# Own slots for ScalarE's reads, value heads stored by group, keys loaded in parts: a two-stage attention block

## What is computed

```python
x = x + _L0_conv_ref(_gn(x), L0_conv_qkv_w, L0_conv_rpb, L0_conv_proj_w, L0_conv_proj_b)
t = _to_tokens(x)
t = t + _L1_attn_ref(_ln_t(t), L1_attn_Wq, L1_attn_bq, L1_attn_Wk, L1_attn_bk, L1_attn_Wv, L1_attn_bv, L1_attn_Wo, L1_attn_bo)
t = t + _L1_ffn_ref(_ln_t(t), L1_ffn_qidx, L1_ffn_scales, L1_ffn_W)
x = _from_tokens(t, x)
```

```python
scores = jnp.einsum("bhqd,bhkd->bhqk", q, k) * scale
weights = jax.nn.softmax(scores, axis=-1)
attn = jnp.einsum("bhqk,bhkd->bhqd", weights, v)
```

## Time and profile before

| | us |
|---|---|
| timed runs, median of 3 | 9913.16 |
| timed runs, lowest and highest | 9905.24, 9916.07 |
| the profiled execution | 9896.01 |
| its span, first to last instruction | 9894.2 |
| front of image 0, alone | 0 to about 486 |
| images 0 to 7 start at | 607, 1774, 2975, 4189, 5390, 6596, 7804, 9012 |

### The profile page before, as it was taken

One profiled execution on the slowest core, in us unless ns is written; L12 is line 12 of the kernel. 1 busy time (PEld: TensorE's weight loads), 2 busy tenths in 40 slices (PEclk: granted clock), 3 DMA queues, 4 the chain that ended last, 5 costly groups with the idle time before them and its releaser, 6 DMA issues.

```text
span 9894.2 us, 433953 instructions
## 1 busy us (share of the span) xinstructions
PE 8886.0 (90%) x173506; PEld 4454.4 (45%) x173506; DVE 7894.2 (80%) x14135; ACT 6501.4 (66%) x13345; POOL 1827.8 (18%) x1913
## 2 busy tenths in 40 slices
PE   4679999999999999999999999999999999999998
PEld 3434444444444444444444444444444444444553
DVE  4478888888887888788888888878888788888996
ACT  1236666666676666666667666666666666667777
POOL 4402221022211222012220122201222022220000
PEclk8779999999999999999999999999999999999999
DMA  3331112211122111221113111121111311112000
GB/s 58 61 53 27 33 35 40 46 31 33 32 38 48 33 31 32 47 39 32 32 35 56 25 33 33 35 53 32 31 31 34 58 29 31 34 29 45 8 10 8
DMA packets 499353, 354.25 MB, mean 36 GB/s; under 512 B 105820, under 2 KB 489036, under 8 KB 495308
## 3 DMA queue, kind: packets, MB, share of 16 engines
q1 hardware_dynamic: 497356, 325.95, 18.4%
HBM read 233.15 MB, written 78.05 MB: 31 GB/s over the span
## 4 chain that ended last, share of the span: by engine, by line
PE 78%; issue 10%; DVE 6%; ACT 3%; SPq 2%; POOL 1%; DVEq 0%; DMA 0%; ACTq 0%; POOLq 0%
PE PS L943 21%; PE PS L1020 19%; PE PS L1005 19%; PE PS L773 6%; PE PS L815 6%; PE PS L824 4%; DVE block_max L1448 3%; PE PS L834 2%; ACT PB L1221 1%; SPq L564 1%; DVE PVM L1333 1%; ACT tail L1141 1%; PE PS L797 0%; POOL SC L682 0%; DVE SUMS L1323 0%
## 5 line engine op out<-in xcount | busy, mean ns | idle before, releaser
L1221 ACT ACTIVATE PB<-PS 128x448 f32<-128x448 f32 (+1 forms) x11200 | 5471.3, 544 | 2532.6 <-PE PS L1005 2508.3
L1448 DVE TENSOR_REDUCE block_max<-PS 128x1 f32<-128x448 f32 x10878 | 6146.8, 616 | 926.9 <-PE PS L943 861.2
L943 PE MATMUL PS<-KP,QP 96*32 96x448 bf16 x43904 | 4199.0, 360 | 238.5 <-issue 106.1
L1005 PE MATMUL PS<-QP,KP 99*32 99x448 bf16 x43904 | 4216.5, 356 | 92.9 <-issue 49.6
L1020 PE MATMUL PS<-PB,VA 128*32 128x448 f32 x22400 | 2698.1, 545 | 34.6 <-issue 32.8
L943 PEld LDWEIGHTS PS<-KP,QP 96*32 96x32 bf16 x43904 | 1291.4, 96 | 1979.6 <-DVE block_max L1448 837.2
L1005 PEld LDWEIGHTS PS<-QP,KP 99*32 99x32 bf16 x43904 | 1309.2, 97 | 1311.4 <-issue 572.0
L1020 PEld LDWEIGHTS PS<-PB,VA 128*32 128x32 f32 x22400 | 736.6, 111 | 399.4 <-issue 63.9
L682 POOL TENSOR_TENSOR SC<-SC,NM 128x1120 f32<-128x1120 f32 x224 | 461.9, 2062 | 2034.7 <-DVE NM L1319 2034.7
L687 POOL TENSOR_TENSOR SC<-SC,SUMS 128x1120 f32<-128x1120 f32 x224 | 462.0, 2062 | 1990.2 <-DVE SUMS L1328 1990.2
L815 PE MATMUL PS<-Kn,QB 32*32 32x80 f32 x25088 | 622.9, 237 | 204.7 <-issue 76.8
(11 more groups left out here) (99 smaller groups left out, 3801.0 us busy)
## 6 DMA issues: line engine op xcount, KB each, us to landing
VP<-vT_padded SPq DMA_DIRECT2D x1792, 70.0 KB
KP<-k_dram SPq DMA_DIRECT2D x96, 392.0 KB, 13.6
QP<-q_dram SPq DMA_DIRECT2D x672, 56.0 KB, 2.1
k_dram<-k_parts SPq DMA_DIRECT2D x56, 336.0 KB, 4.8
q_dram<-q_parts SPq DMA_DIRECT2D x56, 336.0 KB, 3.1
VA<-v_dram SPq DMA_DIRECT2D x16, 816.0 KB, 22.7
vT_padded<-VTs SPq DMA_DIRECT2D x112, 112.0 KB
out_y<-X SPq DMA_DIRECT2D x56, 224.0 KB, 2.0
```

The costliest lines, as they stand in the source:

```text
L943: ins = mm(PS[at:at + QT, bank, 0:BLK], QP[0:ROWS, Q_SLOTS[k % AUNITS], t:t + QT], KP[0:ROWS, g, t // BLK, j * BLK:(j + 1) * BLK], start=T ...
L1005: ins = mm(PS[k0:k0 + 32, bank, 0:BLK], KP[0:ROWSM, k // NBLK, h, c * P + k0:c * P + k0 + 32], QP[0:ROWSM, Q_SLOTS[k], h * BLK:(h + 1) * B ...
L1221: S.activation(exp_buffer(k, c)[0:n, h, :], PS[0:n, at % ST_BANKS, 0:BLK], ACT.Exp, scale=float(ADIM) ** -0.5).then_inc(exp_done, 1)
L1448: V.tensor_reduce(block_max[:, q, j:j + 1], PS[:, bank, 0:BLK], AX.X, ALU.max).then_inc(max_read, 1)
```

## The change

Four edits, most of them in the Plan and in SP's program:

1. negate_max moves from slot (t + 22, 0) to (t + 21, 1) and invert from (t + 2, 0) to (t + 1, 1): the slots in which PE runs turn_max and spread.
2. The DRAM copy of the value heads gets the group as its outermost dimension. store_v2 writes each group by itself (4 DMAs instead of 2 per block; a partition's run in DRAM is 3 x 68 columns, in SBUF it is three pieces of 68). load_v reads one run of 24 x 68 columns (6528 bytes) per partition, instead of 24 pieces of 272 bytes.
3. The keys of group 0 of a new image are loaded in 7 parts (load_k0), one per block of 448 tokens, each of 6 DMAs of 64 rows of 896 bytes; a part stands at least 4 slots behind the key product of its block and at slot 179 + 5 j or later, and waits for the landing of store_k(j).
4. The keys of group 1 are loaded in 6 parts (load_k1), one per stacked part, at slots 4, 14, 24, 34, 44 and 54 instead of all at 2.

```diff
@@ class Plan
-                    self.fix(t + MAX_CHUNKS + 1, 0, "negate_max", k + 1)
+                    self.fix(t + MAX_CHUNKS, 1, "negate_max", k + 1)
...
-                self.fix(2, 0, "load_k", 1)
+                for n in range(len(K_PARTS)):
+                    self.fix(4 + 10 * n, 1, "load_k1", n)
                 self.fix(2, 0, "load_v", 1)
...
             self.fix(t + 1, 1, "spread", k)
-            self.fix(t + 2, 0, "invert", k)
+            self.fix(t + 1, 1, "invert", k)
...
             self.fix(t + 3, 0, "store_k", j)
+            self.fix(max(t + 4, NBLK * CHUNKS + 4 + 5 * j), 1, "load_k0", j)
...
-        self.fix(t + 4, 1, "load_k", 0)
-        self.fix(t + 4, 1, "load_v", 0)
+        self.fix(t + 5, 1, "load_v", 0)
@@ SP
-    v_dram = nc.dram_tensor("v_dram", (images, P, CHUNKS, GROUPS, VCOLS), F32, kind="Internal").ap()
+    v_dram = nc.dram_tensor("v_dram", (images, GROUPS, P, CHUNKS, VCOLS), F32, kind="Internal").ap()
...
                 def store_v2(j):
...
-                    sp.dma_start(dst[:, c + whole[0]:c + whole[1], :],
-                                 VS[:, whole[0]:whole[1], :, :].rearrange("p c h e -> p c (h e)")).then_inc(v_out, 16)
...
+                    for g in range(GROUPS):
+                        dst = image_of(v_dram, b, ahead)[:, g, :, :, :].rearrange("b p c e -> (b p) c e")
+                        heads = slice(g * GH, (g + 1) * GH)
+                        sp.dma_start(dst[:, c + whole[0]:c + whole[1], :],
+                                     VS[:, whole[0]:whole[1], heads, :].rearrange("p c h e -> p c (h e)")
+                                     ).then_inc(v_out, 16)
...
-                def load_k(g):
-                    of_image = ahead if g == 0 else 0
-                    wait(sp, k_out, of(b, of_image, 16 * NBLK, 16 * NBLK))
+                def load_k0(j):
+                    arrived(k_out, of(b, ahead, 16 * NBLK, 16 * (j + 1)))
                     if ahead == 1:
-                        wait(sp, st_ready, of(b, 0, AUNITS * GH * CHUNKS, (1 - g) * NBLK * GH * CHUNKS))
+                        arrived(st_ready, of(b, 0, AUNITS * GH * CHUNKS, NBLK * GH * CHUNKS))
                     for n, m in enumerate(K_PARTS):
-                        src = image_of(k_dram, b, of_image)[:, m, g * GH * ADIM:(g + 1) * GH * ADIM, :] \
+                        src = image_of(k_dram, b, ahead)[:, m, 0:GH * ADIM, j * BLK:(j + 1) * BLK] \
                             .rearrange("b (h e) t -> e (b h) t", e=ADIM)
-                        sp.dma_start(KP[n * ADIM:(n + 1) * ADIM, g, :, :], src).then_inc(keys_in[g], 16)
+                        sp.dma_start(KP[n * ADIM:(n + 1) * ADIM, 0, :, j * BLK:(j + 1) * BLK], src).then_inc(keys_in[0], 16)
+
+                def load_k1(n):
+                    arrived(k_out, of(b, 0, 16 * NBLK, 16 * NBLK))
...
+                    sp.dma_start(KP[n * ADIM:(n + 1) * ADIM, 1, :, :], src).then_inc(keys_in[1], 16)
...
                 def load_v(g):
...
-                    sp.dma_start(dst[:, 0:CHUNKS - 1, :], src[:, 0:CHUNKS - 1, g, :]).then_inc(heads_in[g], 16)
...
+                    cut = (CHUNKS - 1) * VCOLS
+                    sp.dma_start(VA[:, g, 0:cut], src[:, 0:cut]).then_inc(heads_in[g], 16)
```

More of the change, by code:

```diff
@@ L348, in wait @@
                 eng.wait_ge(s, value)
-            if eng is nc.sync and not isinstance(value, int):
-                apart(eng)
         def apart(eng):
@@ L450, in _, with arrived @@
         def _(sp):
+            def arrived(s, value):
+                wait(sp, s, value)
+                if not isinstance(value, int):
+                    apart(sp)
             def load(dst, src):
@@ L511, in store_v1 @@
                     if j == 0:
-                        wait(sp, pv_in, of(b, ahead, STRIPS, 0))
-                    wait(sp, vT_out, of(b, ahead, 32 * NBLK, 32 * j))
-                    wait(sp, v1_read, of(b, ahead, NBLK, j + 1))
+                        arrived(pv_in, of(b, ahead, STRIPS, 0))
+                    arrived(vT_out, of(b, ahead, 32 * NBLK, 32 * j))
+                    arrived(v1_read, of(b, ahead, NBLK, j + 1))
                     for r in range(2):
@@ L521, in load_windows @@
                     row = window_row(s)
-                    wait(sp, vT_out, of(b, ahead, 32 * NBLK, 32 * ((row + WI - 1) // BLOCK_ROWS + 1)))
-                    wait(sp, pv_in, of(b, ahead, STRIPS, s))
+                    arrived(vT_out, of(b, ahead, 32 * NBLK, 32 * ((row + WI - 1) // BLOCK_ROWS + 1)))
+                    arrived(pv_in, of(b, ahead, STRIPS, s))
                     for ky in range(WI):
@@ L535, in store_v2 @@
                 def store_v2(j):
-                    wait(sp, v2_read, of(b, ahead, NBLK, j + 1))
+                    arrived(v2_read, of(b, ahead, NBLK, j + 1))
                     c = 7 * j // 2
@@ L539, in store_v2 @@
                     rows = slice(0, P // 2) if j % 2 == 0 else slice(P // 2, P)
-                    dst = image_of(v_dram, b, ahead).rearrange("b p c g e -> (b p) c (g e)")
-                    sp.dma_start(dst[:, c + whole[0]:c + whole[1], :],
-                                 VS[:, whole[0]:whole[1], :, :].rearrange("p c h e -> p c (h e)")).then_inc(v_out, 16)
-                    sp.dma_start(dst[rows, c + half:c + half + 1, :],
-                                 VS[rows, half:half + 1, :, :].rearrange("p c h e -> p c (h e)")).then_inc(v_out, 16)
@@ L546, in load_k @@
-                def load_k(g):
-                    of_image = ahead if g == 0 else 0
-                    wait(sp, k_out, of(b, of_image, 16 * NBLK, 16 * NBLK))
+                    for g in range(GROUPS):
[4 more added lines that the diff above has]
+                                     ).then_inc(v_out, 16)
+                        sp.dma_start(dst[rows, c + half:c + half + 1, :],
+                                     VS[rows, half:half + 1, heads, :].rearrange("p c h e -> p c (h e)")
+                                     ).then_inc(v_out, 16)
@@ L594, in store_out @@
                 def store_out(i):
-                    wait(sp, ffn_out, of(b, third(i), NBLK, i + 1))
+                    arrived(ffn_out, of(b, third(i), NBLK, i + 1))
                     dst = image_of(yv, b, third(i)).rearrange("b c t -> (b c) t")
@@ L609, in do @@
                         store_v2(i)
-                    elif task == "load_k":
-                        load_k(i)
+                    elif task == "load_k0":
+                        load_k0(i)
+                    elif task == "load_k1":
+                        load_k1(i)
                     elif task == "load_v":
@@ L631, in _ @@
                         do(task, i)
-            do("load_k", 1)
+            for n in range(len(K_PARTS)):
+                do("load_k1", n)
             do("load_v", 1)
@@ L1361, in v2 @@
                     dve.wait_ge(v2_in, of(b, ahead, NBLK, j + 1))
-                    wait(dve, v_out, of(b, ahead, 32 * NBLK, 32 * j))
+                    wait(dve, v_out, of(b, ahead, 64 * NBLK, 64 * j))
                     c0, rows, half = (0, slice(0, P // 2), 3) if j % 2 == 0 else (1, slice(P // 2, P), 0)
```

39 lines of the change are left out of this document (22 added, 17 removed).

## The result

| | before | after |
|---|---|---|
| timed, median (lowest to highest), us | 9910.58 (9905.24 to 9916.07), 4 runs | 9612.20 (9608.69 to 9619.32), 4 runs |
| span of the profiled execution, us | 9894.2 | 9612.8 |
| granted TensorE clock, mean | 0.972 | 0.977 |

The ratio is 0.9699, 95% interval 0.9684 to 0.9714. In the code of after, the lines have moved: scores L1026 (was L1005), max tiles L962 (L943), values L1041 (L1020), exponentials L1242 (L1221), the two of invert L1162 and L1164 (L1141, L1143), negate_max L1155 (L1134), side products L792, L816, L834, L843 and L853 (L773, L797, L815, L824 and L834).

What follows compares the result with a forecast made beforehand. PE's order was taken to bound the kernel, through its standstills. Gains of 150 + 58 + 32 + 20 less 6 made 254 us: 9896 to 9642 profiled, plus 17, about 9660 us as median, range 9590 to 9755.

Steps and rivals of the forecast that it cites:

- The reads in their own slot: ScalarE reads the side bank before its exponential, ending most of PE's 186.7 us of waits: gain 150 us, from 90 to 180.
- sign rows: PE's waits for tail and shift, 186.7 us, should read below 30; its waits for exponentials (PB) should rise by about 10.
- tail and shift: PE's waits until ScalarE has read the spread sums (77 waits, 106.5 us) and the turned maxima (70 waits, 80.2 us).
- the rows of the third norm: Reads already in their own slot, where PE waits 0.24 us each; taken as the price of a moved spread-sums read, 18.5 us.
- Rival A: PE finds late exponentials in most units, not only where its next slot is empty: time about 9716 us; chance 0.15.
- The stop at chunk 316: PE's stop for issue there in images 0 to 6 goes with small key parts and long value runs: 58 us, 30 to 61.
- The stops at the start of an image: PE's stops for issue of 4.0 to 7.0 us, once in images 1 to 7, partly go: gain 32 us, 10 to 54.
- New small stops: Key parts issued one at a time may each still catch a code load: charge 6 us, from 0 to 30.
- The first attention: PE's single 58.9 us wait for queries behind key and value loads shrinks to near 39: gain 20 us, 8 to 30.
- Queues passed: SP's added key issues, value stores and waits for store_k should fit into its existing waits; no term in the sum.
- Rival C: SP becomes the bound: key parts delay window loads; slower from about 7.9 us a part, 10,069 us at 12.8; chance 0.03.
- Rival B: The bulk stops stay, because any large copy (X) delays the code or parts merely spread it: 9743 us; chance 0.12.

Runs made afterwards that it cites:

- the kernel with the loads at once: Changed kernel with all six key parts of group 1 at slot 2, back to back as before the change: 9655.2 us, ratio 0.9740.
- the burst: Changed kernel with all seven parts of group 0 (42 DMAs, rows of 896 bytes) issued straight after one another: 9681.2 us, ratio 0.9758.

## Why the prediction was right in kind and 48 us high

The working of the forecast is compared term by term, with the change in chunk times as the measure. The sum was 254 us; 281 came in the span. The other 20 of the 48 us lie around the span: I added 17 between profile and median, and the median of after is 2.7 us below its profiled execution (9614.9). That the 27 us of the span are so few is partly luck: the start of an image gave 25 us more than forecast, the reads 11 and chunk 316 7, and 17 us more than forecast went to new stops.

- **The reads in their own slot: 150 forecast, 161 measured** (159 by the medians of the kernel that has them alone). The mechanism and its sign rows came as told. Two sizes were off, in opposite directions: the rest that I left to tail and shift, 25 us by the rows of the third norm, is zero, since a read that stands ahead of the exponential is over before PE's slot; and PB rose by 20, not 10 (16 alone). The row of the third norm was a poor neighbour: a quarter of a microsecond there was not the price of a read in its own slot. Rival A, late exponentials everywhere, falls: it asked for 60 us more of waits for PB, and there are 20, partly repaid.
- **The stop at chunk 316: 58 forecast, 65.5 measured.** All seven went. 65.5 less the 47.5 of the stops leaves 18 us for the clock behind them and small waits, where I took 10.5. That PE's code is late, an assumption there, is shown by the transfers of the instruction queue. The cause of the lateness as given, bulk in flight, was too broad: the key loads in one burst make it, the value load does not.
- **The stops at the start of an image: 32 forecast, some 57 measured** (58.8 by chunk times, 56 by the kernel with the loads at once). This is the term that was sized worst, by 25 us, and it lies above its range, which ended at 54; the term of chunk 316 lies above its range too, 65.5 against 61. I added up 16 us of bulk that remains there, by landings, and let half of the stops stay. Bytes were the wrong measure: what remains, a value load and one key load, never stopped PE at chunks 3 and 6, although the load of X there lands in 10.0 us. By rows it could have been read: the six key loads have 384 rows of 6272 bytes, 24 for each of the 16 DMA engines if they are dealt out evenly, and land in 21.9 us, an estimate of 0.9 us a row, and the packets give 0.88; one load has four such rows an engine.
- **New small stops: 6 forecast, 23 measured** (25 at chunk 39, and 2 us of gain elsewhere). Inside the 0 to 30 given. The charge assumed that the parts of group 1 come one at a time. They don't: slots order SP's queue, they don't hold it back.
- **The first attention: 20 forecast, 19.6 measured**, the wait for queries 38.4 where 39 stood. The agreement to half a microsecond is luck: in the kernel with the reads alone, whose front is unchanged, attention starts 5.1 us earlier than in before.
- **Queues passed: nothing forecast, nothing seen.** Rival C falls. In the front alone SP waits 8.3 us for landings of keys, over 3 times, and the front ends as before; beside attention the 42 issues don't appear in PE's waits. They do as soon as they are not spread (23.94 us, the burst).
- **Rival B, that stops stay,** falls for chunk 316 and for chunks 3 and 6; it holds in a small way for the copy into X, which in blocks gives back 13 us at chunks 0 and 1. The stop of about 3 us left at the last chunk of five images is not of a copy: it stays with the copy in blocks, and stands where the loop jumps back.

The rule of the Trainium skill (DMA: Bandwidth & Descriptors, Queues, rings and completion order), by which a single part could hold a code load for four long descriptors at most, gave a charge of 0 for single parts. Where no other part is near (the first three and the last of each image) the trace agrees, with no stop over 2.4 us beside it; where two go out 3.8 to 5.1 us apart it does not, with stops of 2.9 to 4.6 us in four of six images. The other rule of the Trainium skill that was weighed, that loads under 64 KB pay mostly overhead (Rules for kernel authors, same page), is borne out by the burst: 42 issues of 56 KB held SP for 23.94 us where six of 392 KB took 2.73 (in the kernel with the value heads alone). In the change this time is there too and hidden.

## What to carry to other kernels

If an engine stops "for issue" while loads are in flight, look for the loads whose rows hold the DMA engines longest (here keys, 0.88 us a row against 0.25 for a value row of more bytes), not for those that hold the issuing queue longest or have the most bytes: issuing the keys in short rows, spread out, took the stop away and hid the cost of the issues. A reader of a shared bank belongs in the slot of its writer, ahead of longer work of its engine; the lateness this puts on that work was mostly repaid a chunk later in the last image, the one place where that was measured. A slot in a plan is an order and no date: if a DMA must not go out early, something has to hold it.

## What the runs showed of the hardware that was not expected

- Six key loads with 64 rows of 6272 bytes each stop PE for 4 to 8 us, and then its granted clock is 0.50 for some microseconds; the same bytes in rows of 896 bytes don't, though they keep the queue busy for 24 us. A load of 816 KB in pieces of 272 bytes, which held SP for 20.54 us, had no part in the stops.
- A stop of PE for issue of 2 us or more ends 1.2 to 2.2 us after a 16 KB transfer of the instruction queue (382 of 383 stops); the jump back of the hardware loop costs one of 2.7 to 3.3 us each time.
- A key row of 6272 bytes takes a DMA engine 0.88 us with six loads in flight and 0.63 with one beside values and X, a value row of 6528 bytes 0.25, a row of X of 10752 bytes 0.41. Engines 94% busy at 253 GB/s with values and X did not stop PE; engines full at 121 GB/s with key rows did.
- Two such key loads 3.8 to 5.1 us apart, with a window load between them, stopped PE for 2.9 to 4.6 us in four of six images and not in the other two; in rows of 1568 bytes the four stops are still there, 2.4 to 2.6 us. In images 3 and 4, without a stop, a transfer of code begins 4.6 and 4.1 us after the second load is issued; in the four others the next one begins 8.6 to 11.3 us after it. Why it gets through early in two of six is open.
- The load of X (1344 KB) went from 6.4 to 10.0 us by what now stands beside it, and PE did not see it.
- Waits for issue of 2 to 3.4 us move from place to place with every edit of the loads, and their sum stays (54 us in after, 48 to 69 in seven variants); some 15 us of it are the loop's five jumps back. The rest was neither explained nor removed.
